# A batched Gram matrix with packed lower triangles: one TensorE loop of 43 laps, three slots to a set of banks, a group's halves consecutive, stores by 32 rows, first loads held apart

## The chip, the cores and the metric

One core of a Trainium2 chip (trn2) runs the program. The metric is the device time of one execution in microseconds (us), the median over several runs. TensorE (PE), VectorE (DVE), ScalarE (ACT) and GpSimd (POOL) compute; SyncE (SP) only issues DMAs here. The engines run their own instruction streams and meet at semaphores.

## The reference

The input is 2048 matrices of 64 rows and 256 columns (float32, 134 MB). For each matrix the kernel computes all products of pairs of rows and writes those below the diagonal, packed (2016 numbers for each matrix, 16.5 MB in all).

```python
Z = jnp.einsum('bnd,bmd->bnm', inputs, inputs)      # 2048 x 64 x 64
li, lj = jnp.tril_indices(64, k=-1)
return Z[:, li, lj]                                 # 2048 x 2016
```

## The kernel before, in words

The work goes by tiles of 16 matrices, 128 tiles in all. A tile has two sides of 8 matrices (side 0 ends on partitions 0 to 63, side 1 on 64 to 127), and each side has two slots of 4 matrices. Eight tiles make a group of 128 matrices, and there are 16 groups.

- SP (`load`, L99): one DMA of 1 MB for each tile, 128 partitions by 4 rows of 2 KB, into `x_in`, a ring of 8 tiles. The load of tile t waits until tile t-8 is turned.
- DVE (`turn`, L156): one 32x32 block transpose of a whole tile from `x_in` to `x_turned`, a ring of 3 tiles. It waits for the load and for the products of tile t-3.
- PE (`multiply`, L199): 256 matmuls for each tile, 128 for each slot (8 chunks of 32 columns by 4 quadrants by 2 sides), each preceded by its weight load. Slot s has its own four banks `slot_banks{s}`, and its next use waits until ACT has copied the last one. The first two tiles (128 % 3 = 2, `BEFORE_LOOP`) are written out ahead of a loop of 42 laps of 3 tiles.
- ACT (`keep`, L221): one copy of 128x256 from the banks to `products` for each slot; `products` holds two groups. From tile 10 on ACT also does, after each `keep`, a quarter of a piece of `pack` (L236, L239): it copies the rows of a turned group to their packed places in `packed_rows`, which has two buffers. A group has 4 pieces of 16 rows and so 16 quarters. The first quarter of a group waits until the store of the group before the last has landed (`stored`), and ACT's later `keep`s stand behind that wait.
- DVE (`turn_rows`, L170): four transposes of 128x1024 for each group, `PIECE_LAG` = 10 tiles and more behind, from `products` to `row_halves`.
- POOL (L141): 62 small copies for each group, 31 rows by 2 sides, that carry the columns from 32 on across 32 partitions; before its last two pieces are done SP can't store.
- SP (`store`, L105, L110): after the load of tile 8g+28 (`STORE_LAG`) it waits for ACT and POOL and issues four DMAs of 252 KB for group g, one for each run of 32 positions and each side. Stores and loads stand in one queue. The rows of y that belong to one side of a tile are 8 consecutive ones, and then 8 of the other side follow, so a store is written as

```python
rows = y[first:first + BLOCK * SIDES].rearrange("(t s u) c -> s t u c", s=SIDES, u=PER_SIDE)
sync.dma_start(rows[side], packed_rows[side * HALF:side * HALF + BLOCK, buffer, run])
```

with t = 4 as its outermost dimension and u = 8 under it.

Of the kernel before, what the change touches and what calls it, by code (L numbers as in the profile page):

```python
# [7 lines left out]
PARTS = 128  # L8
# [11 lines left out]
def gram_lower_triangle(nc: bass.Bass, x: bass.AP, y: bass.AP):  # L20
# [5 lines left out]
    TILE = QUADRANTS * SIDES * SLOTS  # L26
    TILES = BATCHES // TILE
    PER_SIDE = QUADRANTS * SLOTS
    IN_RING = 8
    RING = 3  # L30
    BANKS = 4
    ARRAY_TILES = QUADRANTS * SIDES


    BEFORE_LOOP = TILES % RING
    LATE_CHUNK = CHUNKS - 2


    GROUP_TILES = 8
    GROUP = GROUP_TILES * TILE  # L40
    GROUPS = TILES // GROUP_TILES
    KEPT = GROUP // SIDES
    RUNS = KEPT // BLOCK
    PIECES = 4
    PIECE = ROWS // PIECES
# [3 lines left out]
    PIECE_LAG = GROUP_TILES + 2  # L49
    STORE_LAG = PIECE_LAG + 2 * PIECES + 2 + IN_RING  # L50
# [4 lines left out]
    with ExitStack() as stack:  # L55
# [3 lines left out]
        def semaphore(name):  # L59
# [3 lines left out]
        x_turned = sbuf("x_turned", [PARTS, RING, SIDES * SLOTS, CHUNKS, ROWS])  # L63
        products = sbuf("products", [PARTS, 2, ROWS, KEPT])
# [4 lines left out]
        banks = [stack.enter_context(nc.psum_tensor(f"slot_banks{s}", [PARTS, BANKS, 8, ROWS], F32))  # L69
                 for s in range(SLOTS)]  # L70

        loaded = [semaphore(f"loaded{k}") for k in range(IN_RING)]
        turned = [semaphore(f"turned{j}") for j in range(RING)]
        multiplied = [semaphore(f"slot_multiplied{s}") for s in range(SLOTS)]
        kept = [[semaphore(f"kept{j}_{s}") for s in range(SLOTS)] for j in range(RING)]
        rows_turned = semaphore("rows_turned")
        packed_home = semaphore("packed_home")
        packed_across = semaphore("packed_across")
        stored = [semaphore(f"stored{b}") for b in range(2)]

        block = stack.enter_context(nc.Block())


        turned_ahead = [RING if j >= BEFORE_LOOP else 0 for j in range(RING)]
        kept_ahead = [(turned_ahead[j], RING if j + 1 >= BEFORE_LOOP else 0) for j in range(RING)]

        def turned_value(t):
            return turned_ahead[t % RING] + (t // RING + 1) * RING

        def kept_value(t, slot):  # L90
            return kept_ahead[t % RING][slot] + (t // RING + 1) * RING

        @block.sync
        def _(sync):
            def load(t):
                k = t % IN_RING
                if t >= IN_RING:
                    sync.wait_ge(turned[(t - IN_RING) % RING], turned_value(t - IN_RING))
                sync.dma_start(x_in[:, k], x_pairs[t * TILE * BLOCK:(t + 1) * TILE * BLOCK].rearrange(  # L99
                    "(k p) e -> p k e", p=PARTS)).then_inc(loaded[k], 16)  # L100

            def store(group):
                buffer = group % 2
                sync.wait_ge(packed_home, (group + 1) * PIECES)
                sync.wait_ge(packed_across, (group + 1) * (PIECES // 2))  # L105
                for run in range(RUNS):
                    first = group * GROUP + run * BLOCK * SIDES
                    rows = y[first:first + BLOCK * SIDES].rearrange("(t s u) c -> s t u c", s=SIDES, u=PER_SIDE)
                    for side in range(SIDES):
                        sync.dma_start(rows[side], packed_rows[side * HALF:side * HALF + BLOCK, buffer, run]).then_inc(  # L110
                            stored[buffer], 16)

            for t in range(TILES):
                load(t)
                group, behind = divmod(t - STORE_LAG, GROUP_TILES)
                if group >= 0 and behind == 0:
                    store(group)
            for group in range((TILES - 1 - STORE_LAG) // GROUP_TILES + 1, GROUPS):
                store(group)
            for b in range(2):  # L120
                sync.wait_ge(stored[b], (GROUPS - b + 1) // 2 * SIDES * RUNS * 16)

        @block.gpsimd
        def _(pool):
            for j in range(RING):
                if turned_ahead[j]:
                    pool.sem_inc(turned[j], turned_ahead[j])
                for slot in range(SLOTS):
                    if kept_ahead[j][slot]:
                        pool.sem_inc(kept[j][slot], kept_ahead[j][slot])  # L130

            for group in range(GROUPS):
                buffer = group % 2
                if group >= 2:
                    pool.wait_ge(stored[buffer], group // 2 * SIDES * RUNS * 16)
                for piece in range(PIECES // 2, PIECES):
                    pool.wait_ge(rows_turned, group * PIECES + piece + 1)  # L137
                    for i in range(max(BLOCK + 1, piece * PIECE), (piece + 1) * PIECE):
                        for side in range(SIDES):
                            first = side * HALF  # L140
                            last = nc.gpsimd.tensor_copy(  # L141
                                packed_rows[first:first + BLOCK, buffer, :,
                                            first_column(i) + BLOCK:first_column(i) + i],
                                row_halves[first + BLOCK:first + HALF, i, :, 0:i - BLOCK])
                    last.then_inc(packed_across, 1)

        @block.vector
        def _(dve):
            def turn(t):


                k, j = t % IN_RING, t % RING
                dve.wait_ge(loaded[k], (t // IN_RING + 1) * 16)
                if t >= RING:
                    dve.wait_ge(multiplied[SLOTS - 1], (t - RING + 1) * ARRAY_TILES)  # L155
                nc.vector.transpose(  # L156
                    x_turned[:, j].rearrange("p k c (i r) -> p k r c i", r=JOINED),
                    x_in[:, k].rearrange("p k (r c d) -> p k r c d", r=JOINED, c=CHUNKS)).then_inc(turned[j], RING)

            def turn_rows(group, piece):  # L160
                rows = slice(piece * PIECE, (piece + 1) * PIECE)
                if piece == 0:
                    last = (group + 1) * GROUP_TILES - 1
                    dve.wait_ge(kept[last % RING][SLOTS - 1], kept_value(last, SLOTS - 1))
                if group > 0:

                    dve.wait_ge(packed_home, (group - 1) * PIECES + piece + 1)  # L167
                    if piece >= PIECES // 2:
                        dve.wait_ge(packed_across, (group - 1) * (PIECES // 2) + piece - PIECES // 2 + 1)
                nc.vector.transpose(  # L170
                    row_halves[:, rows].rearrange("p i h j -> p (i h) j"),
                    products[:, group % 2, rows, :].rearrange("p i (h q) -> p (i h) q", q=BLOCK)).then_inc(
                    rows_turned, 1)

            for t in range(TILES):
                turn(t)
                group, behind = divmod(t - PIECE_LAG, GROUP_TILES)
                if group >= 0 and behind % 2 == 0:
                    turn_rows(group, behind // 2)
            for n in range((TILES - 1 - PIECE_LAG) // 2 + 1, GROUPS * PIECES):  # L180
                turn_rows(n // PIECES, n % PIECES)

        @block.tensor
        def _(pe):
            def multiply(j, step, first_of_all=False):


                pe.wait_ge(turned[j], step)
                for slot in range(SLOTS):
                    if slot > 0 and not first_of_all:  # L190
                        pe.wait_ge(kept[(j - 1) % RING][slot], step)
                    for c in range(CHUNKS):
                        if slot == SLOTS - 1 and c == LATE_CHUNK:

                            pe.wait_ge(kept[j][0], step)
                        for g in range(QUADRANTS):
                            for side in range(SIDES):
                                rows = x_turned[g * BLOCK:(g + 1) * BLOCK, j, side * SLOTS + slot, c, :]
                                done = nc.tensor.matmul(  # L199
                                    banks[slot][side * HALF:(side + 1) * HALF, g, 0, :], rows, rows,  # L200
                                    start=c == 0, stop=c == CHUNKS - 1)
                                if c == CHUNKS - 1:
                                    done.then_inc(multiplied[slot], 1)

            for t in range(BEFORE_LOOP):
                multiply(t, RING, first_of_all=t == 0)
            laps = TILES // RING
            with pe.Fori(2 * RING, (laps + 2) * RING, RING) as step:
                for n in range(RING):
                    multiply((BEFORE_LOOP + n) % RING, step)  # L210

        @block.scalar
        def _(act):
            def keep(t, slot):
                group, in_group = divmod(t, GROUP_TILES)
                if group >= 2 and in_group == 0 and slot == 0:

                    act.wait_ge(rows_turned, (group - 1) * PIECES)
                act.wait_ge(multiplied[slot], (t + 1) * ARRAY_TILES)  # L219
                first = in_group * PER_SIDE + slot * QUADRANTS  # L220
                nc.scalar.copy(products[:, group % 2, :, first:first + QUADRANTS],  # L221
                               banks[slot][:, :, 0, :].rearrange("p g i -> p i g")).then_inc(kept[t % RING][slot], RING)

            def pack(n, quarter):

                group, piece = divmod(n, PIECES)
                buffer = group % 2
                if piece == 0 and quarter == 0 and group >= 2:
# [40 lines left out]
```

## Time and profile before

| | |
|---|---|
| median of 3 runs | 545.54 us (545.45, 545.54 and 549.28) |
| profiled execution, its own time | 549.26 us |
| its span, first to last instruction | 547.5 us |
| PE / weight loads / DVE / ACT / POOL busy | 417.1 / 408.4 / 359.7 / 206.5 / 202.9 us |
| granted TensorE clock, mean | 0.903 of full speed |
| moved by DMA | 151.09 MB, 276 GB/s over the span |

The busy times are sums over the whole span, which has three stretches with different limits: the first 60 us, the tiles after them, and the last 36 us, in which PE has nothing to do. PE's busy time is modelled and says little of how fast it goes; the distance between laps is the better measure.

### The profile page before, as it was taken

The numbers are of one execution on the slowest core, as the hardware profiler recorded it, in microseconds if no ns is written. First come the engines' busy times: TensorE is split into PE (matmuls) and PEld (weight loads), VectorE is DVE, ScalarE is ACT, GpSimd is POOL, SyncE is SP. The second block draws the span as 40 slices with busy tenths as digits, with TensorE's granted clock in tenths as the row PEclk, the third lists the DMA queues.
The fourth block names the chain that finished last, engine by engine and source line by source line (L and its number), as shares of the span: only waits on it lengthen the run. The fifth ranks groups of instructions, "written<-read, shape, count | busy, mean of one in ns | idle before, by whom it ended". The sixth has DMA issues, their size and how long they took to land.

```text
span 547.5 us, 68554 instructions
## 1 busy us (share of the span) xinstructions
PE 417.1 (76%) x32768; PEld 408.4 (75%) x32768; DVE 359.7 (66%) x192; ACT 206.5 (38%) x1009; POOL 202.9 (37%) x996
## 2 busy tenths in 40 slices
PE   2345799999999895969779695978969596997300
PEld 2335799999999895969779695978969595997300
DVE  4213489999898593949669393967949395785300
ACT  1001125554555452534344352435435252443710
POOL 0000006372826080624417071442608053361880
PEclk9999999999999997988979798897979798797755
DMA  8982499999796997979798897969799797974011
GB/s 312 386 305 88 167 349 331 325 320 341 270 351 244 331 329 264 339 244 360 239 339 302 286 335 257 331 231 365 281 308 322 245 332 284 328 261 161 25 75 76
DMA packets 69921, 151.09 MB, mean 276 GB/s; under 512 B 2304, under 2 KB 2304, under 8 KB 69888
## 3 DMA queue, kind: packets, MB, share of 16 engines
q1 hardware_dynamic: 69888, 150.74, 78.0%
q8 instruction: 10, 0.16, 0.1%
q14 instruction: 23, 0.19, 0.1%
HBM read 134.22 MB, written 16.52 MB: 275 GB/s over the span
## 4 chain that ended last, share of the span: by engine, by line
DMA 36%; PE 36%; SPq 9%; issue 7%; POOL 5%; DVE 3%; ACT 2%; POOLq 0%; DVEq 0%; ACTq 0%
PE slot_banks L199 36%; DMA y_dram<-packed_rows 22%; DMA x_in<-x_dram 14%; POOL packed_rows L141 5%; SPq L110 4%; SPq L99 4%; DVE x_turned L156 3%; ACT packed_rows L236 1%; ACT products L221 1%; DVE row_halves L170 1%; POOLq L55 0%; DVEq L155 0%; ACTq L219 0%; DVEq L167 0%; POOLq L137 0%
## 5 line engine op out<-in xcount | busy, mean ns | idle before, releaser
L199 PE MATMUL slot_banks<-x_turned 32*64 32x64 f32 x32768 | 417.1, 247 | 93.8 <-ACT products L221 52.5
L199 PEld LDWEIGHTS slot_banks<-x_turned 32*64 32x64 f32 x32768 | 408.4, 140 | 102.3 <-ACT products L221 54.0
L156 DVE STREAM_TRANSPOSE x_turned<-x_in 128x2048 f32<-128x2048 f32 x128 | 291.0, 2289 | 152.9 <-DMA x_in<-x_dram 65.8
L141 POOL COPY packed_rows<-row_halves 32x2 f32<-32x2 f32 (+30 forms) x992 | 202.7, 204 | 331.9 <-DVE row_halves L170 291.8
L221 ACT COPY products<-slot_banks 128x256 f32<-128x256 f32 x256 | 95.2, 372 | 235.8 <-PE slot_banks L199 235.8
L236 ACT COPY packed_rows<-row_halves 128x2 f32<-128x2 f32 (+30 forms) x496 | 71.2, 220 | 67.5 <-DMA y_dram<-packed_rows 67.4
L170 DVE STREAM_TRANSPOSE row_halves<-products 128x1024 f32<-128x1024 f32 x64 | 76.9, 1203 | 8.6 <-POOL packed_rows L141 4.9
L239 ACT COPY packed_rows<-row_halves 128x128 f32<-128x128 f32 x256 | 63.2, 303 | 1.9 <-DVE row_halves L170 1.9
L221 ACT ACT_TABLE_LOAD x1 | 1.3, 1283 | 11.2 <-PE slot_banks L199 11.2
L263 POOL MEMSET const-float32-0.0<- 128x1 f32 x1 | 0.1, 98 | 0.2 <-issue 0.2
L263 POOL MEMSET const-bfloat16-1.0<- 128x1 bf16 x1 | 0.1, 101 | 0.0
L263 POOL MEMSET const-uint8-127<- 128x1 uint8 x1 | 0.1, 99 | 0.0
L263 POOL MEMSET const-float32-1.0<- 128x1 f32 x1 | 0.1, 98 | 0.0
## 6 DMA issues: line engine op xcount, KB each, us to landing
x_in<-x_dram SPq DMA_DIRECT2D x128, 1024.0 KB, 15.4
y_dram<-packed_rows SPq DMA_DIRECT2D x64, 252.0 KB
```

The lines of the kernel that those rows point to most:

```text
L99: sync.dma_start(x_in[:, k], x_pairs[t * TILE * BLOCK:(t + 1) * TILE * BLOCK].rearrange("(k p) e -> p k e", p=PARTS)).then_inc(loaded[k], 16)
L110: sync.dma_start(rows[side], packed_rows[side * HALF:side * HALF + BLOCK, buffer, run]).then_inc(stored[buffer], 16)
L141: last = nc.gpsimd.tensor_copy(packed_rows[first:first + BLOCK, buffer, :, first_column(i) + BLOCK:first_column(i) + i], row_halves[first ...
L156: nc.vector.transpose(x_turned[:, j].rearrange("p k c (i r) -> p k r c i", r=JOINED), x_in[:, k].rearrange("p k (r c d) -> p k r c d", r=J ...
L170: nc.vector.transpose(row_halves[:, rows].rearrange("p i h j -> p (i h) j"), products[:, group % 2, rows, :].rearrange("p i (h q) -> p (i ...
L199: done = nc.tensor.matmul(banks[slot][side * HALF:(side + 1) * HALF, g, 0, :], rows, rows, start=c == 0, stop=c == CHUNKS - 1)
L221: nc.scalar.copy(products[:, group % 2, :, first:first + QUADRANTS], banks[slot][:, :, 0, :].rearrange("p g i -> p i g")).then_inc(kept[t ...
L236: last = nc.scalar.copy(packed_rows[:, buffer, :, at:at + i], row_halves[:, i, :, 0:i])
L239: last = nc.scalar.copy(two[:, :, :, 0:BLOCK], row_halves[:, i:i + 2].rearrange("p w h j -> p h w j"))
L263: nc = bacc.Bacc("TRN2", target_bir_lowering=False, num_devices=1)
```

## The change

PE's program becomes one loop of 43 laps of three tiles. As 43 times 3 is 129, the first lap begins with a blank tile that DVE fills with zeros. The banks are now two sets of four; the six slots of a lap are put in them three by three (`SET_SLOTS` = 3), and ACT copies a set at once (or in two copies, where a group ends inside it). `products` holds three groups instead of two. A tile now has 8 matrices of the first half of its group and 8 of the second half, so one side of a group is 64 consecutive matrices: a load is two DMAs of 512 KB, and a store of a group is two DMAs of 64 rows of y, written with 32 as outermost dimension. Among the first loads, those of tiles 2, 3 and 4 wait until the load before has landed. Pieces go from the last rows to the first. `PIECE_LAG` goes from 10 to 11, a piece's packing from 21 slots behind to 23, `STORE_LAG` from 28 to 30. In the last group DVE carries side 1 across and POOL only side 0; POOL packs the 15 shortest rows; and the group is stored in two parts, rows 32 to 63 first.

```diff
+    APART = range(2, 5)
+    LAP = 3
+    LAPS = -(-TILES // LAP)
+    BLANK = LAPS * LAP - TILES
+    SETS = 2
+    SET_SLOTS = LAP * SLOTS // SETS
...
+    KEPT_RING = 3
...
-    PIECE_LAG = GROUP_TILES + 2
-    STORE_LAG = PIECE_LAG + 2 * PIECES + 2 + IN_RING
+    PIECE_LAG = GROUP_TILES + 3
+    PACK_LAG = 2 * PIECE_LAG + 1
+    STORE_LAG = PIECE_LAG + 2 * PIECES + 3 + IN_RING
...
                 if t >= IN_RING:
-                    sync.wait_ge(turned[(t - IN_RING) % RING], turned_value(t - IN_RING))
-                sync.dma_start(x_in[:, k], x_pairs[t * TILE * BLOCK:(t + 1) * TILE * BLOCK].rearrange(
-                    "(k p) e -> p k e", p=PARTS)).then_inc(loaded[k], 16)
...
+                    lap, j = place(t - IN_RING)
+                    sync.wait_ge(turned[j], (lap + 1) * LAP)
+                elif t in APART:
+
+                    sync.wait_ge(loaded[t - 1], SIDES * 16)
+                group, in_group = divmod(t, GROUP_TILES)
+                for side in range(SIDES):
+                    first = (group * GROUP + side * KEPT + in_group * PER_SIDE) * BLOCK
+                    sync.dma_start(x_in[:, k, side * SLOTS:(side + 1) * SLOTS],
+                                   x_pairs[first:first + PER_SIDE * BLOCK].rearrange("(k p) e -> p k e", p=PARTS)
+                                   ).then_inc(loaded[k], 16)
+
+            def store(group, columns):
+                for side in range(SIDES):
+                    first = group * GROUP + side * KEPT
+                    sync.dma_start(y[first:first + KEPT, columns].rearrange("(h q) c -> q h c", q=BLOCK),
+                                   packed_rows[side * HALF:side * HALF + BLOCK, group % 2, :, columns]).then_inc(
+                        stored[group % 2], 16)
...
+            group, long_rows = GROUPS - 1, first_column(BLOCK)
+            sync.wait_ge(packed_home, group * PIECES + LONG_PIECES)
+            sync.wait_ge(packed_across, (group + 1) * LONG_PIECES)
+            sync.wait_ge(last_carried, 1)
+            store(group, slice(long_rows, PACKED))
+            sync.wait_ge(packed_home, GROUPS * PIECES - 1)
+            sync.wait_ge(last_packed, 1)
+            store(group, slice(0, long_rows))
...
+            for j in range(BLANK):
+                nc.vector.memset(x_turned[:, j], 0.0).then_inc(turned[j], LAP)
...
+            for i in range(BLOCK + 1, ROWS):
+                last = carry_across(nc.vector.tensor_copy, GROUPS - 1, i, 1)
+            last.then_inc(last_carried, 1)
...
+                for slot in range(SLOTS):
+                    s, at = divmod(j * SLOTS + slot, SET_SLOTS)
+                    if s == 1 and at == 0:
+                        pe.wait_ge(kept[1], step)
                     for c in range(CHUNKS):
-                        if slot == SLOTS - 1 and c == LATE_CHUNK:
...
+                        if j == LAP - 1 and slot == SLOTS - 1 and c == CHUNKS - 2:
+
+                            pe.wait_ge(kept[0], step)
...
-            for t in range(BEFORE_LOOP):
-                multiply(t, RING, first_of_all=t == 0)
-            laps = TILES // RING
-            with pe.Fori(2 * RING, (laps + 2) * RING, RING) as step:
-                for n in range(RING):
-                    multiply((BEFORE_LOOP + n) % RING, step)
...
+            with pe.Fori(LAP, (LAPS + 1) * LAP, LAP) as step:
+                for j in range(LAP):
+                    multiply(j, step)
...
+                    if group >= KEPT_RING and in_group == 0:
+
+                        act.wait_ge(rows_turned, (group - KEPT_RING + 1) * PIECES)
```

## Rows read from the trace of the kernel before

**Rows 1.** The page, 40 slices of the span, busy tenths of PE and DMA.
```profile
PE   2345799999999895969779695978969596997300
DMA  8982499999796997979798897969799797974011
```

**Rows 2.** Chain that ended last, 60 to 165 us: start us, us, what.
```profile
69.39 9.06 PE slot_banks L199 x413
...
78.60 9.13 PE slot_banks L199 x433
...
87.89 9.06 PE slot_banks L199 x415
```

**Rows 3.** The page, groups of instructions: busy us, mean ns | idle before, releaser.
```profile
L156 DVE STREAM_TRANSPOSE x_turned<-x_in 128x2048 f32<-128x2048 f32 x128 | 291.0, 2289 | 152.9 <-DMA x_in<-x_dram 65.8
L141 POOL COPY packed_rows<-row_halves 32x2 f32<-32x2 f32 (+30 forms) x992 | 202.7, 204 | 331.9 <-DVE row_halves L170 291.8
L221 ACT COPY products<-slot_banks 128x256 f32<-128x256 f32 x256 | 95.2, 372 | 235.8 <-PE slot_banks L199 235.8
...
L170 DVE STREAM_TRANSPOSE row_halves<-products 128x1024 f32<-128x1024 f32 x64 | 76.9, 1203 | 8.6 <-POOL packed_rows L141 4.9
```

**Rows 4.** Windows: stretch, length, PE, PEld, DVE, ACT, POOL, PEclk, DMA share, GB/s.
```profile
10.00:30.00 20.00, 8.28 (x482) 7.84 (x477) 6.16 (x4) 2.46 (x5) 0.00 (x0) 1.00 1.05 389
...
70.00:100.00 30.00, 29.57 (x2533) 29.18 (x2520) 27.73 (x15) 13.12 (x62) 12.07 (x60) 1.00 0.98 342
...
174.50:177.50 3.00, 3.00 (x281) 3.00 (x265) 2.39 (x2) 1.55 (x7) 0.60 (x3) 1.00 0.26 108
185.00:195.00 10.00, 9.23 (x796) 8.96 (x781) 9.64 (x6) 5.24 (x30) 3.77 (x21) 1.00 1.03 378
...
245.00:250.00 5.00, 5.00 (x341) 5.00 (x332) 3.01 (x2) 1.97 (x13) 0.00 (x0) 0.50 1.00 356
```

**Rows 5.** Loads issued at 62 to 88 us (ns of SP, landing), then 178 to 199 us.
```profile
L99 SPq DMA_DIRECT2D x_in<-x_dram x9: 367/368/368, 62.3 to 87.7; - x9
...
DMA to landing us min/median/max: 5.2/5.3/6.3
...
DMA to landing us min/median/max: 14.0/16.9/21.7
```

**Rows 6.** Waits of PE and of ACT, whole span: us, times, longest.
```profile
PE slot_banks L199 <- ACT products L221: 52.5, 11, 5.8
...
ACT packed_rows L236 <- DMA y_dram<-packed_rows: 67.4, 11, 7.2
```

**Rows 7.** The page, DMA packets of the span, and the queue of PE's code.
```profile
DMA packets 69921, 151.09 MB, mean 276 GB/s; under 512 B 2304, under 2 KB 2304, under 8 KB 69888
...
q8 instruction: 10, 0.16, 0.1%
```

**Rows 8.** Timeline of PE in the first 60 us: start, us, group [idle before].
```profile
8.71 3.73 PE L199 MATMUL slot_banks<-x_turned 32*64 32x64 f32 x223 [8.71 <-DVE x_turned L156]
...
16.18 2.35 PE L199 MATMUL slot_banks<-x_turned 32*64 32x64 f32 x128 [3.74 <-issue]
...
43.79 2.34 PE L199 MATMUL slot_banks<-x_turned 32*64 32x64 f32 x128 [1.39 <-issue]
...
58.81 11.40 PE L199 MATMUL slot_banks<-x_turned 32*64 32x64 f32 x860 [3.29 <-issue]
```

**Rows 9.** Timeline of the end, 499 us on.
```profile
499.64 11.20 PE L199 MATMUL slot_banks<-x_turned 32*64 32x64 f32 x865
...
504.69 30.37 POOL L141 COPY packed_rows<-row_halves 32x2 f32<-32x2 f32 x124 [15.51 <-DVE row_halves L170]
...
513.92 3.79 ACT L236 COPY packed_rows<-row_halves 128x2 f32<-128x2 f32 x31
517.62 1.69 ACT L239 COPY packed_rows<-row_halves 128x128 f32<-128x128 f32 x8
...
535.15 3.61 SPq L110 DMA_DIRECT2D y_dram<-packed_rows  x4
```

More of the change, by code:

```diff
@@ L97, in load, with store_whole @@
                 if t >= IN_RING:
-                    sync.wait_ge(turned[(t - IN_RING) % RING], turned_value(t - IN_RING))
-                sync.dma_start(x_in[:, k], x_pairs[t * TILE * BLOCK:(t + 1) * TILE * BLOCK].rearrange(
-                    "(k p) e -> p k e", p=PARTS)).then_inc(loaded[k], 16)
-            def store(group):
-                buffer = group % 2
-                sync.wait_ge(packed_home, (group + 1) * PIECES)
[L105 to L111, printed above, removed]
+                    lap, j = place(t - IN_RING)
[14 more added lines that the diff above has]
+                        stored[group % 2], 16)
+            def store_whole(group):
+                sync.wait_ge(packed_home, (group + 1) * PIECES)
+                sync.wait_ge(packed_across, (group + 1) * LONG_PIECES)
+                store(group, slice(0, PACKED))
             for t in range(TILES):
@@ L124, in _ @@
         def _(pool):
[L125 to L130, printed above, removed]
+            pool.sem_inc(kept[1], LAP)
             for group in range(GROUPS):
[L133 to L136, printed above, removed]
+                last_group = group == GROUPS - 1
+                wait_packed_free(pool, group)
+                for piece in range(LONG_PIECES):
@@ L137, in _ @@
                     pool.wait_ge(rows_turned, group * PIECES + piece + 1)
[L138 to L144, printed above, removed]
@@ L145, in _ @@
-                    last.then_inc(packed_across, 1)
+                    rows = piece_rows(piece)
+                    for i in range(max(BLOCK + 1, rows.start), rows.stop):
+                        for side in range(1 if last_group else SIDES):
+                            last = carry_across(nc.gpsimd.tensor_copy, group, i, side)
+                    last.then_inc(packed_across, 1)
+            pool.wait_ge(packed_across, GROUPS * LONG_PIECES)
+            pool.wait_ge(rows_turned, GROUPS * PIECES)
@@ L147, in _ @@
+            rows = piece_rows(PIECES - 1)
+            for i in range(1, rows.stop):
+                last = pack_short(nc.gpsimd.tensor_copy, GROUPS - 1, i)
+            last.then_inc(last_packed, 1)
         @block.vector
@@ L157, in turn, with turn_rows @@
                     x_turned[:, j].rearrange("p k c (i r) -> p k r c i", r=JOINED),
[L158 to L161 removed]
+                    x_in[:, k].rearrange("p k (r c d) -> p k r c d", r=JOINED, c=CHUNKS)).then_inc(turned[j], LAP)
+            def turn_rows(n):
+                group, piece = divmod(n, PIECES)
+                rows = piece_rows(piece)
@@ L175, in _ @@
+            turned_rows = 0
             for t in range(TILES):
                 turn(t)
[L177 to L181, printed above, removed]
+                if t >= PIECE_LAG and (t - PIECE_LAG) % 2 == 0:
+                    turn_rows(turned_rows)
+                    turned_rows += 1
@@ L212, in _ @@
         @block.scalar
         def _(act):
[L214 to L228, printed above, removed]
-                    act.wait_ge(stored[buffer], group // 2 * SIDES * RUNS * 16)
+            def keep(lap, s):
+                act.wait_ge(half_multiplied if s == 0 else tile_multiplied[LAP - 1], (lap + 1) * ARRAY_TILES)
+                begin = (lap * SETS + s) * SET_SLOTS - BLANK * SLOTS
+                slot, end = max(0, begin), begin + SET_SLOTS
+                while slot < end:
+                    group, in_group = divmod(slot, GROUP_SLOTS)
+                    count = min(end - slot, GROUP_SLOTS - in_group)
+                    if group >= KEPT_RING and in_group == 0:
+                        act.wait_ge(rows_turned, (group - KEPT_RING + 1) * PIECES)
+                    last = nc.scalar.copy(
+                        products[:, group % KEPT_RING, :, in_group * QUADRANTS:(in_group + count) * QUADRANTS].rearrange(
+                            "p i (m g) -> p i m g", g=QUADRANTS),
+                        bank_sets[s][:, :, slot - begin:slot - begin + count, :].rearrange("p g m i -> p i m g"))
+                    slot += count
+                last.then_inc(kept[s], LAP)
@@ L230, in pack @@
+            def pack(n):
+                group, quarter = divmod(n, PIECES * 4)
+                piece, quarter = divmod(quarter, 4)
+                if piece == 0 and quarter == 0:
+                    wait_packed_free(act, group)
                 if quarter == 0:
-                    act.wait_ge(rows_turned, n + 1)
-                first = piece * PIECE + quarter * (PIECE // 4)
+                    act.wait_ge(rows_turned, group * PIECES + piece + 1)
+                first = piece_rows(piece).start + quarter * (PIECE // 4)
@@ L241, in pack @@
                 if quarter == 3:
                     last.then_inc(packed_home, 1)
-            behind = 0
-            for t in range(TILES):
-                for slot in range(SLOTS):
-                    keep(t, slot)
-                    if 2 * t + slot > 2 * PIECE_LAG:
-                        pack(behind // 4, behind % 4)
-                        behind += 1
-            for n in range(behind, GROUPS * PIECES * 4):
-                pack(n // 4, n % 4)
+            n = 0
+            for lap in range(LAPS):
+                for s in range(SETS):
+                    keep(lap, s)
+                    while n + PACK_LAG < (lap * SETS + s + 1) * SET_SLOTS - BLANK * SLOTS:
+                        pack(n)
+                        n += 1
@@ L256 @@
+            for n in range(n, (GROUPS * PIECES - 1) * 4):
+                pack(n)
 def kernel(r_inputs):
```

106 lines of the change are left out of this document (62 added, 44 removed).

## The prediction

> **What bounds the kernel now.** I began with the slices of the page [rows 1]: PE is half idle in the first four slices, full in the next nine, and then dips at even distances to the end; in the last three it does nothing. So there are three stretches, each to be read by itself.
>
> *The full stretch* shows what PE can do. On the chain of work that ended last, laps of three tiles start at 69.39, 78.60 and 87.89 us [rows 2]: 9.21 and 9.29 us, 3.07 to 3.10 us for a tile. Two tiles and one `turn_rows` cost DVE 2 x 2.29 + 1.20 = 5.8 us against 6.1 of PE, and two `keep`s cost ACT 0.74 [rows 3]. PE is the bound there, and the DMA engines follow it with 342 GB/s [rows 4]; a load lands 5.3 us after its issue, so the input ring is full [rows 5].
>
> *The dips*: PE waits 52.5 us for ACT's copies, and ACT waits 67.4 us, 11 times, for a store to land before it may pack [rows 6]. Why does a store land late? While stores are moved, the DMA share is 0.26 and the rate 108 GB/s, against 1.03 and 378 GB/s beside it [rows 4]. A quarter of the engines works, four of sixteen, and the loads behind stand still. The packet count says the same: 2304 small packets [rows 7] are 128 loads x 16 + 64 stores x 4. The outermost dimension is 128 for a load and 4 for a store. A group's four stores, 1.03 MB, at 108 GB/s take 9.6 us; on sixteen engines, at four times that, 2.4 us. Over this the loads fall behind, they land 17 us after issue [rows 5], and the store in the same queue does too. PE idles, comes back at half its clock (0.50, the 1.2 GHz level [rows 4]) and loses some more.
>
> *The start*: PE runs 223 matmuls, stops 3.74 us, then runs 128 at a time in 2.35 us with stops of 1.39 to 4.3 us that nothing in the trace releases; there are 9 from 12.44 to 58.81 us, and then none [rows 8]. 128 matmuls and their weight loads are 256 instructions, half a tile. PE's queue of code has 10 pieces, 0.16 MB, thus 16 KB each [rows 7], which is 64 bytes for each of those 256. Two written-out tiles and a first lap of three are ten half tiles. So each stop is code arriving once.
>
> *The end*: PE is done at 510.84. POOL carries 124 rows from 504.69 to 535.06, SP issues the last stores until 538.76, and the span ends at 547.5 [rows 9]: 36.7 us behind PE.
>
> **The change part by part.**
>
> 1. *Start.* Code for three tiles instead of five: 6 half tiles. The 223 matmuls that PE has at once are 1.75 of them, so 4.25 must come, in five pieces. PE needs no input for the blank tile: the memset of 2048 elements isn't in the trace; it lies between nothing and a transpose of the same tile, 2.3 us, and I take 2 (it is the same size), so PE starts at about 3 us and runs dry at 3 + 3.7 = 6.7 [rows 8]. A piece costs its 2.35 us plus a stop: 1.39 with little traffic, 3.3 around a single load, 3.7 to 4.3 under full traffic [rows 8]. Loads 2 to 4 are held apart, so I take 3.3 for three stops, 4 for two: 6.7 + 3 x 3.3 + 2 x 4 + 4 x 2.35 + 0.6 = 34.6, call it 34 us for the end of lap 1, with two real tiles done. All stops cheap give 6.7 + 5 x 1.4 + 10 = 24, all dear 38. The price of holding apart is idle DMA time: three lone loads at 5.3 us instead of some 2.7 [rows 4, 5], 8 us. PE's code covers it: load 1 is there at 8 us, load 4 at 8 + 3 x 5.3 = 24, load 8 at 24 + 4 x 2.7 = 35, while PE at 34 us needs only the third tile.
>
> 2. *Middle.* 42 laps remain. With the stores at 32 outermost rows I take sixteen engines, the even split, as the row of the loads has it; the other bound is four, as now (a rival below). DMA work of a group: eight loads of 1 MB at 378 to 389 GB/s [rows 4], 21.6 to 22.2 us, plus 2.4 us: 24.0 to 24.6, against 8 x 3.07 to 3.10 = 24.6 to 24.8 of PE. That is hardly less, but PE is still the longer, and the ring holds eight tiles. So PE's lap of 9.21 to 9.29 stays: 42 x 9.24 = 388 us. The clock stays full when no wait breaks it, as in 70 to 100 us.
>  The Trainium skill, page "DMA: Bandwidth & Descriptors", section "Why a DMA increments its semaphore by 16 and not by 1", says that a DMA uses the largest number of engines up to 16 that divides the outermost dimension on both sides. By that rule the old store gets four and the new one sixteen; the trace agrees for 4 and 128, and no run so far shows 32.
>
>  *Waits added or moved.* Two load DMAs for a tile: SP spends 0.37 us on one of 1 MB [rows 5], so at most 0.74, under 3.07; SP isn't late. `keep` for three slots: 128x768 isn't in the trace; between 0.37 (one slot) and 3 x 0.37 = 1.12 us [rows 3]; I take 0.75, two-thirds of it being elements. Either is under the three slots, 4.6 us, in which the other set fills, and ACT's total falls or stays. The store of group g is issued after load 8g+30, at about PE's tile 21.4 of those counted from 8g, as ACT finishes packing near 21; behind SP's wait stand loads 8g+31 and on, at most 2 tiles late, while the ring holds 8: hidden, unless the queue is empty and DMA has no spare, which leads to the second rival. ACT's packing of group g+2 needs the store when tile 28 to 29 is kept: 6.6 to 7.6 tiles or 20 to 23 us after issue. In a short queue a store lands in 5.3 us, in a deep one in 17 to 22 [rows 5]. So this wait goes where PE is the bound. What is late next is PE itself. The third buffer of `products` takes away a wait that the trace doesn't show as a cost: nothing. Blank tile: in the first lap, counted.
>
> 3. *End*, from PE's last matmul on (E). ACT copies the last set, E + 0.8, and then has 22 quarters of packing: of group 14 the last 4 long copies (L239) and 31 short ones (L236), of group 15 16 and 16, at 1.69/8 = 0.21 and 3.79/31 = 0.12 us each [rows 9]: 20 x 0.21 + 47 x 0.12 = 9.8, E + 11. POOL takes (30.37 us for 124 copies, with a wait; 0.204 each plus a gap, 0.25 [rows 3, 9]) until about E + 2.5 for group 14, then 31 copies of side 0, 7.8 us, then 15 short rows, 3.6 us: E + 14. DVE has four `turn_rows` (E + 7.5, each waiting for ACT's piece) and 31 copies; such copies on DVE aren't in the trace, so between nothing and POOL's 0.25 us each, I take ACT's 0.12, the nearest row: E + 11.3. So the long rows' store is issued at E + 11.3 and the short rows' at E + 14, two issues at 3.61/4 = 0.9 us each [rows 9], and it lands some 2.6 later, what a lone load takes beyond its bytes: E + 18. Bounds: E + 14 to E + 23. Before it was 36.7: the gain is 31 carries off POOL, no four-engine store at the end, and less in the last store.
>
> **Sum.** 34 + 388 + 18 = 440 us of span. The profiled execution before had 547.5 of span in 549.26 of its own time, 1.8 more: 442. That execution lay 3.7 above the median of its three runs, where the other two are; the changed kernel should have less of such waiting, so I take half of it off: 440 us, about -19%. By part: start, lap 1's end and the tiles done set against each other, (60.9 - 5 x 3.08) - (34 - 2 x 3.08) = 17.7; end 18.7; the rest, 71, in the middle.
>
> **Rivals.**
>
> - *The DMA engines become the bound* (0.18). For it: 342 GB/s already at a share of 0.98 in the stretch where they only follow PE [rows 4], so the spare may be far less than 389 suggests; stores add to it. 150.7 MB at 342 GB/s are 441 us, plus 5 for the start, minus 6 for stores that fall in the end, plus a transpose and a tile's products 5, plus 18: 463. Against: 378 GB/s for 10 us in the middle, with full use of PE and DVE. It decides from where eight loads take more than 24.7 - 2.4 us, which is 376 GB/s, near to the 378 of [rows 4]; every 10 GB/s below cost some 10 us in all, so the first of them lie within the forecast's own range.
>  The Trainium skill, same page, section "Specifications", gives some 358 GB/s of HBM for a core; an estimate by it would be 421 us for the bytes and some 443 in all. The rows of 378 and 389 GB/s speak against it as a limit of a core alone.
> - *ACT still waits for stores* (0.08). The landing, not the bandwidth, sets it: if it takes over 6.6 tiles, each of 12 groups waits. Half the present 6.1 us [rows 6] for each is 37: 477.
> - *Stores stay on four engines* (0.05): the change then doesn't do what it says. The middle keeps its present (510.84 - 60.9)/123 = 3.66 us a tile: 34 + 126 x 3.66 + 18 = 513.
> - *Slower than before* (0.03): a pair of half loads isn't overlapped with its neighbours as one whole load is, because the queue admits so many DMAs, not so many bytes. A lone load takes 5.3 us [rows 5]; at that for a tile the middle is 126 x 5.3 = 668, in all 720. It decides from (547.5 - 34 - 18)/126 = 3.9 us a tile. Against it: now loads stand six deep, so that three would do.
>
> **How the numbers follow.** The forecast has 0.66: 440, its own range 426 to 455 from start 24 to 38, laps of 9.18 to 9.4, end 14 to 23. With the first two rivals 0.92 is covered up to 480, and the low end of all bounds together is 424. Under 1% is what a measurement of this kernel can't tell from no change; no case lies there, 0.02 is kept for it, 0.03 for slower.
>
> **What would show it.** Start: PE's code queue with about 6 pieces, not 10; PE busy from about 3 us; steady laps from 24 to 38 us. Middle: laps 9.2 us apart to the end, clock 1.00, no slice near 0.26 of DMA share, small packets as many as 256 x 16 for loads and 16 for each of some 34 stores; ACT's wait for stores near zero. If DMA bounds: DVE waits for loads throughout, share near 1, landing 15 us and more. End: 18 us behind PE. The prediction is wrong if stores of 32 rows don't spread, or if PE's lap with three slots in one bank isn't the lap of before: the trace can't show that.

## The result and the profile after

The changed kernel takes 437.28 us (436.77 to 437.67, 4 runs) against 545.5 us, a ratio of 0.800 (0.797 to 0.804). The forecast was 440. The profiled execution has 435.9 us of span.

The page of the changed kernel, 40 slices of the span; they answer to [rows 1], a slice now being 10.9 us:

```profile
PE   4569999999999999999998999989899998989810
...
DMA  5589999999999999999999999999999999999416
```

The first line is the row of busy tenths of PE, the second that of DMA. The dips at even distances are gone from both. DMA is at 9 from the fourth slice to the 37th without a break, which it never was for long before, and PE has small gaps in the second half. The same page, counts and queues (to [rows 7]), and groups of instructions (to [rows 3]):

```profile
DMA packets 72378, 151.01 MB, mean 346 GB/s; under 512 B 4640, under 2 KB 4768, under 8 KB 72352
...
q8 instruction: 6, 0.10, 0.1%
...
L282 ACT COPY products<-bank_set 128x768 f32<-128x768 f32 (+2 forms) x96 | 69.0, 729 | 215.4 <-PE bank_set L256 204.9
...
L122 DVE COPY packed_rows<-row_halves 32x2 f32<-32x2 f32 (+30 forms) x31 | 3.5, 191 | 0.0
L225 DVE MEMSET x_turned<- 128x2048 f32 x1 | 1.8, 1765 | 1.2 <-PEq L325 1.2
```

4640 small packets are 256 x 16 for the loads and 34 x 16 for the stores: every DMA now ends on sixteen engines. Six pieces of code come instead of ten.

The timeline of PE at the start (to [rows 8]); the bracket is the idle time before:

```profile
3.05 3.70 PE L256 MATMUL bank_set<-x_turned 32*64 32x64 f32 x222 [3.05 <-DVE x_turned L225]
...
9.89 2.35 PE L256 MATMUL bank_set<-x_turned 32*64 32x64 f32 x128 [3.14 <-issue]
...
27.83 17.42 PE L256 MATMUL bank_set<-x_turned 32*64 32x64 f32 x1384 [2.85 <-issue]
```

The laps after it, on the chain from 30 to 70 us (to [rows 2]):

```profile
38.41 8.78 PE bank_set L256 x425
47.19 0.12 issue
47.31 8.78 PE bank_set L256 x424
```

A lap takes 8.90 us here, against 9.21. Counted back from the one that starts at 38.41 - 8.90, lap 1 ends at 29.5 us. The waits of the whole span (to [rows 6]), and windows with the columns of [rows 4]:

```profile
PE bank_set L256 <- DVE x_turned L203: 10.7, 14, 1.8
...
DVE x_turned L203 <- DMA x_in<-x_dram: 41.5, 15, 4.2
...
ACT packed_rows L117 <- DMA y_dram<-packed_rows: 15.9, 9, 3.6
...
POOL packed_rows L122 <- DMA y_dram<-packed_rows: 132.5, 13, 10.8
```

```profile
30.00:60.00 30.00, 29.59 (x2564) 29.20 (x2555) 24.36 (x13) 4.80 (x6) 4.97 (x24) 1.00 1.05 389
60.00:200.00 140.00, 138.08 (x12097) 135.97 (x12091) 132.49 (x71) 65.86 (x309) 71.04 (x349) 1.00 1.04 385
200.00:300.00 100.00, 94.72 (x8269) 92.72 (x8261) 87.30 (x48) 45.11 (x215) 50.71 (x248) 1.00 1.02 371
...
424.00:427.00 3.00, 0.00 (x0) 0.00 (x0) 2.97 (x11) 2.91 (x19) 3.00 (x21) 0.50 1.00 239
```

PE no longer waits for ACT at all. It waits for DVE, and DVE for loads (12 of the 41.5 us lie in the first 60 us, the others behind them): the DMA engines have become the bound, at 385 to 389 GB/s first and 371 later. The eight tiles loaded ahead hide it until 169 us, where DVE's first wait for a load stands on the chain. And the end (to [rows 9]):

```profile
407.54 20.07 POOL L122 COPY packed_rows<-row_halves 32x32 f32<-32x32 f32 x93 [10.22 <-DMA y_dram<-packed_rows]
...
412.50 2.95 PE L256 MATMUL bank_set<-x_turned 32*64 32x64 f32 x256 [1.05 <-DVE x_turned L203]
```

PE is done at 415.45, and 20.4 us follow. From lap 1's end that makes (415.45 - 29.5)/42 = 9.19 us a lap on average.

### The profile page after: what moved, and what is told of

Read it like the earlier page. It is cut to its first block, busy times and chain, and to the rows that moved or that the text cites. A ratio compares the mean times of both kernels' runs of the same rounds, so it can differ in the third digit from the quotient of the medians.

```text
span 435.9 us, 68822 instructions
## 1 busy us (share of the span) xinstructions
PE 385.4 (88%) x33024; PEld 377.5 (87%) x33024; DVE 363.7 (83%) x224; ACT 179.3 (41%) x834; POOL 197.2 (45%) x980
## 2 busy tenths in 40 slices
DMA packets 72378, 151.01 MB, mean 346 GB/s; under 512 B 4640, under 2 KB 4768, under 8 KB 72352
## 4 chain that ended last, share of the span: by engine, by line
PE 35%; DMA 28%; DVE 16%; SPq 10%; issue 6%; POOL 3%; ACT 0%; DVEq 0%; POOLq 0%
PE bank_set L256 35%; DMA x_in<-x_dram 25%; DVE x_turned L203 12%; SPq L138 9%; DVE row_halves L219 3%; DMA y_dram<-packed_rows 3%; POOL packed_rows L122 3%; DVE packed_rows L122 1%; DVE x_turned L225 0%; SPq L145 0%; ACT packed_rows L117 0%; ACT products L282 0%; DVEq L202 0%; DVEq L218 0%; DVEq L64 0%
## 5 line engine op out<-in xcount | busy, mean ns | idle before, releaser
L256 PE MATMUL bank_set<-x_turned 32*64 32x64 f32 x33024 | 385.4, 237 | 30.0 <-issue 12.1
L256 PEld LDWEIGHTS bank_set<-x_turned 32*64 32x64 f32 x33024 | 377.5, 132 | 37.8 <-issue 21.9
L203 DVE STREAM_TRANSPOSE x_turned<-x_in 128x2048 f32<-128x2048 f32 x128 | 290.6, 2286 | 58.0 <-DMA x_in<-x_dram 41.5
L122 POOL COPY packed_rows<-row_halves 32x60 f32<-32x60 f32 (+30 forms) x961 | 194.9, 204 | 232.3 <-DMA y_dram<-packed_rows 132.5
L282 ACT COPY products<-bank_set 128x768 f32<-128x768 f32 (+2 forms) x96 | 69.0, 729 | 215.4 <-PE bank_set L256 204.9
L117 ACT COPY packed_rows<-row_halves 128x128 f32<-128x128 f32 x256 | 56.4, 300 | 17.4 <-DMA y_dram<-packed_rows 15.9
L111 ACT COPY packed_rows<-row_halves 128x32 f32<-128x32 f32 (+30 forms) x481 | 62.3, 220 | 0.0
L122 DVE COPY packed_rows<-row_halves 32x2 f32<-32x2 f32 (+30 forms) x31 | 3.5, 191 | 0.0
L225 DVE MEMSET x_turned<- 128x2048 f32 x1 | 1.8, 1765 | 1.2 <-PEq L325 1.2
L111 POOL COPY packed_rows<-row_halves 128x2 f32<-128x2 f32 (+14 forms) x15 | 2.1, 195 | 0.1
```

The lines of the kernel that those rows point to most:

```text
L111: return copy(packed_rows[:, group % 2, :, at:at + i], row_halves[:, i, :, 0:i])
L117: return copy(two[:, :, :, 0:BLOCK], row_halves[:, i:i + 2].rearrange("p w h j -> p h w j"))
L122: return copy(packed_rows[first:first + BLOCK, group % 2, :, at + BLOCK:at + i], row_halves[first + BLOCK:first + HALF, i, :, 0:i - BLOCK])
L203: nc.vector.transpose(x_turned[:, j].rearrange("p k c (i r) -> p k r c i", r=JOINED), x_in[:, k].rearrange("p k (r c d) -> p k r c d", r=J ...
L225: nc.vector.memset(x_turned[:, j], 0.0).then_inc(turned[j], LAP)
L256: done = nc.tensor.matmul(bank_sets[s][side * HALF:(side + 1) * HALF, g, at, :], rows, rows, start=c == 0, stop=c == CHUNKS - 1)
```

## The experiments

Times are medians of four runs; ratios are to the kernel before on the same chip. For the changed kernel it is 0.800 (0.797 to 0.804).

**Stores on four engines again** (`e_store4`).

```diff
-                    sync.dma_start(y[first:first + KEPT, columns].rearrange("(h q) c -> q h c", q=BLOCK),
-                                   packed_rows[side * HALF:side * HALF + BLOCK, group % 2, :, columns])...
+                    for run in range(RUNS):
+                        rows = y[first + run * BLOCK:first + (run + 1) * BLOCK, columns]
+                        sync.dma_start(rows.rearrange("(u t) c -> t u c", t=4),
+                                       packed_rows[side * HALF:side * HALF + BLOCK, group % 2, run, columns])...
```

> The changed kernel, but each store is four DMAs with 4 as outermost dimension, as before the change (the 32 rows of a run land in y in another order; all else is computed as it was). Theory A, the spread of the stores over the engines is what the middle gained: the stretches with a DMA share near 0.25 come back for about 9.6 us in each group, ACT waits some 60 us for stores, and the time is 500 to 520 us, against 437. Theory B, the middle gained from the third products buffer, the longer lags and PE's loop, and the engines of a store matter little: 437 to 450 us.

520.67 us, ratio 0.952 (0.947 to 0.956): theory A, just above its upper end. The dips are back in PE's row, and a window shows the quarter share:

```profile
PE   4369999999999695987959699595987959699300
...
226.00:228.00 2.00, 2.00 (x211) 2.00 (x196) 0.00 (x0) 0.00 (x0) 0.00 (x0) 1.00 0.25 105
...
ACT packed_rows L117 <- DMA y_dram<-packed_rows: 69.9, 11, 7.6
```

ACT's wait for stores is 69.9 us in 11 times, as before the change. The third buffer of `products` and the longer lags don't prevent it.

**The kernel before with stores by 32 rows** (`b_spread`). Only `load` and `store` are taken from the change, with their counts.

```diff
-                for run in range(RUNS):
-                    first = group * GROUP + run * BLOCK * SIDES
-                    rows = y[first:first + BLOCK * SIDES].rearrange("(t s u) c -> s t u c", s=SIDES, u=PER_SIDE)
-                    for side in range(SIDES):
-                        sync.dma_start(rows[side], packed_rows[side * HALF:side * HALF + BLOCK, buffer, run])...
+                for side in range(SIDES):
+                    first = group * GROUP + side * KEPT
+                    sync.dma_start(y[first:first + KEPT].rearrange("(h q) c -> q h c", q=BLOCK),
+                                   packed_rows[side * HALF:side * HALF + BLOCK, buffer])...
```

> The kernel before, but a tile has 8 matrices of each half of its group, so that a group is stored by two DMAs with 32 as outermost dimension; PE's program, lags, the banks and the end are as before. Theory A: nearly all of the middle's gain is here, 545 - 73 = 472 us, with laps of 9.2 us and no PE stop longer than 2 us after the start; the end a few us shorter as well, so 462 to 478. Theory B: 530 to 545 us.

465.5 us, ratio 0.851 (0.847 to 0.855): theory A. Row of PE, two waits and the last stretch of PE:

```profile
PE   2336599999999999999999999999999999999500
...
PE slot_banks L202 <- issue: 26.2, 14, 4.1
PE slot_banks L202 <- DVE x_turned L159: 8.4, 1, 8.4
...
416.70 18.25 PE L202 MATMUL slot_banks<-x_turned 32*64 32x64 f32 x1536 [0.17 <-issue]
```

After the start PE never stops for longer than the 0.1 to 0.2 us between laps; it is done at 434.95, and the span of 463.4 ends 28.5 us later. So the stores, with the order of tiles that they need, give some 80 of the 108 us, and the rest of the change 28. The traces tell where these 28 lie. On the chain of this run PE has eight tiles done and begins a lap here:

```profile
67.36 9.07 PE slot_banks L202 x413
```

The changed kernel is that far at 47.31, 20.1 us earlier; it is 19.5 us ahead at PE's last matmul, and its end is 8.0 us shorter (20.4 against 28.5). The start gives 20 us, the end 8, and the laps between give nothing.

**The first lap written out ahead of the loop** (`e_ahead`): 12 half tiles of code instead of 6.

```diff
+            for j in range(LAP):
+                multiply(j, LAP)
-            with pe.Fori(LAP, (LAPS + 1) * LAP, LAP) as step:
+            with pe.Fori(2 * LAP, (LAPS + 1) * LAP, LAP) as step:
```

> The changed kernel with the first lap written out ahead of the loop, so that PE's code is 12 half tiles instead of 6. Theory A, each half tile of code met for the first time costs a stop: 12 pieces in the code queue, steady laps start after some 49 instead of 29 us. As DMA is the bound and loads what it can meanwhile, most of these 20 us but not all reach the end: 8 to 18 us slower. Theory B, the stops at the start come from the first use of banks or from waits, not from code: no change.

457.26 us, 20 more than the changed kernel, ratio 0.836 (0.830 to 0.842). The stops run on to 61 us, and the code queue has twice the pieces:

```profile
q8 instruction: 12, 0.20, 0.2%
...
61.18 14.04 PE L256 MATMUL bank_set<-x_turned 32*64 32x64 f32 x1066 [2.57 <-issue]
...
72.23 8.78 PE bank_set L256 x424
...
430.56 2.95 PE L256 MATMUL bank_set<-x_turned 32*64 32x64 f32 x256 [0.72 <-DVE x_turned L203]
```

Code it is (A), but the 20 us lie above the 8 to 18 expected, because the delay was larger than the 20 us assumed. The last two lines are a lap on the chain and PE's last stretch. Counted back from the lap at 72.23, the first two laps end at 63.3 us, against 38.4 in the profiled execution of the changed kernel: 24.9 us later. PE's last matmul is 18.1 us later, so some 7 us were made up on the way. How much is made up depends on what it is compared with: beside `a_again` (below), the same program as the changed kernel with a slower start, the two distances are 19.8 and 19.3 us.

**The last group as the others** (`e_tail`): POOL carries both sides, DVE none.

> The changed kernel, but in the last group POOL carries both sides and DVE none. POOL has 31 more copies of 0.25 us before it packs the short rows: the end is 6 to 8 us longer, the rest the same, 443 to 445. If another engine sets the end (ACT with its 22 quarters), less than 3 us.

445.35 us, 8 more, ratio 0.814 (0.808 to 0.820), just above the 443 to 445 expected; POOL's last stretch has 124 copies instead of 93.

```profile
406.21 30.37 POOL L122 COPY packed_rows<-row_halves 32x32 f32<-32x32 f32 x124 [10.20 <-DMA y_dram<-packed_rows]
```

The 8 us are those by which the end of `b_spread` is longer. That 437.3 + 20 + 8 also makes the 465.5 us of `b_spread` is in part chance: `e_ahead` has 12 pieces of code and starts PE at 3 us, `b_spread` has the ten of before and starts PE at 8.5 us.

**More increments** (`e_inc6`): the slots that have none at their end increment a semaphore that nobody reads.

```diff
                                     elif at == SET_SLOTS - 1:
                                         done.then_inc(half_multiplied, 1)
+                                    else:
+                                        done.then_inc(unread, 1)
```

> The changed kernel with 16 more semaphore increments in a lap (48, as before the change, instead of 32), on a semaphore that nobody waits for. Theory A, the increments of the last matmuls are why an unhindered lap takes 8.90 us instead of the 9.21 before: the lap becomes 9.2 us, 19 ns for an increment; the total hardly moves, by 0 to 4 us, as DMA takes over as the bound. Theory B, the 5 instead of 9 waits in a lap or the banks' layout made it shorter: the lap stays at 8.90.

438.13 us, ratio 0.801 (0.797 to 0.805), the same time. The chain shows the lap of before again, 9.19 us:

```profile
47.57 9.06 PE bank_set L257 x414
56.64 0.12 issue
56.76 9.06 PE bank_set L257 x414
...
DVE x_turned L204 <- DMA x_in<-x_dram: 21.6, 9, 3.6
```

So theory A: 16 increments cost 0.29 us, 18 ns each; neither the waits nor the layout of the banks had shortened the lap. The last line is from this run's waits of DVE. PE itself waits for no tile after its start here and keeps its laps of 9.19 us to the end, and yet the time is the same: with 48 increments PE's own pace is what the loads allow, and with 32 it is faster than that to no use.

**Fewer bytes** (`e_less`): of every other tile from the ninth on, side 1 is loaded only by half; old contents stand in for the rest.

> The changed kernel, but of every other tile from the ninth on a quarter of the rows isn't loaded (the old contents are used), 15 MB less in 120 tiles. Theory A, from about 30 us on the DMA engines are the bound and PE only spends the eight tiles loaded ahead: laps stay at 8.90 to the end, DVE's waits for loads (41.5 us) go, and the time falls by some 12 us, to 423 to 427. Theory B, PE's later stops come from the order of waits between the engines, not from the rate: laps lengthen after 169 us all the same, 433 to 438.

427.62 us, ratio 0.781 (0.775 to 0.786), some 10 less. PE keeps its lap to the end of the work:

```profile
374.22 8.80 PE bank_set L257 x424
383.14 8.80 PE bank_set L257 x423
```

PE's waits for DVE are gone and DVE's for loads are 6.0 us. The 6.0 us all lie in the first 60 us. Theory A; its 423 to 427 is just missed. In the profiled execution the first lap ended some 5 us later than in the one of the changed kernel; whether that is the reason wasn't tried.

**Three buffers of packed rows, two of products** (`e_packed3`), in the same memory.

```diff
-    KEPT_RING = 3
+    KEPT_RING = 2
+    PACKED_RING = 3
```

(and `group % PACKED_RING` for `packed_rows` and `stored`.)

> The changed kernel with three buffers of packed_rows and two of products (the same memory), so that ACT and POOL wait for the store of three groups back. Theory A, the end is 20.4 us instead of 18 because POOL's last two groups start only when the store of group 12 has landed (at 407.54), behind the deep queue of loads: POOL's waits for stores (132 us) go, group 14 is carried before PE ends, the end falls to 13 to 16 us and the time by 4 to 8. The products buffer given up costs nothing or stops of 1 us in a group. Theory B, the third products buffer matters, as ACT must wait for turned rows: slower by 5 us or more.

433.15 us, ratio 0.791 (0.785 to 0.797), 4 less: theory A. The interval just touches that of the changed kernel; `c1_inc1` below, with the same buffers and fewer increments, is clear of `a_again`. POOL's waits and PE's and POOL's last stretches:

```profile
POOL packed_rows L123 <- DVE row_halves L220: 190.5, 16, 55.7
...
413.50 2.95 PE L257 MATMUL bank_set<-x_turned 32*64 32x64 f32 x256 [0.86 <-DVE x_turned L204]
...
418.93 4.70 POOL L123 COPY packed_rows<-row_halves 32x32 f32<-32x32 f32 x31 [3.09 <-DVE row_halves L220]
```

POOL waits for no store any more, and the span of 432.6 ends 16.2 us behind PE. ACT waits 3.4 us in all for turned rows, since the third buffer of `products` is gone.

**All first loads at once** (`e_noapart`): `APART = range(0)`.

> The changed kernel with the first loads all issued at once. Theory A, the DMA engines are the bound from 30 us on and the 3 x 3.7 us of DMA time given up at the start are missing at the end: the first lap ends some 8 us later (stops of 3.7 to 4.3 us instead of 1.1 to 3.1), yet the time falls by 1 to 5 us. Theory B, PE is the bound, so a later first lap is a later end: slower by 6 to 9 us.

439.38 us, ratio 0.803 (0.799 to 0.807) against 0.800 (0.797 to 0.804): no difference that can be told, and neither expectation holds. Two windows of this kernel, and DVE's waits for loads:

```profile
0.00:30.00 30.00, 11.46 (x650) 10.70 (x657) 11.01 (x5) 1.66 (x2) 0.20 (x4) 1.00 0.97 358
30.00:60.00 30.00, 25.80 (x2116) 25.34 (x2110) 17.89 (x8) 4.25 (x6) 0.00 (x0) 1.00 0.81 287
...
DVE x_turned L203 <- DMA x_in<-x_dram: 19.8, 9, 3.2
```

The loads move 358 instead of 219 GB/s in the first 30 us, but in the next 30 us 287 instead of 389, for the ring of eight is full while PE waits for its code. By 60 us that is 19.4 MB against 18.2: 3 us of loading won. PE's first lap ended at 35.52 + 10.46 - 8.79 = 37.2 us by its stretch on the chain, 7.7 later. Most of it isn't missing at the end: PE, and DVE behind it, start later, and DVE then waits 19.8 us for loads instead of 41.5. The two effects nearly cancel; none was tried alone.

**The three last together**, beside the changed kernel once more (`a_again`). `c1_inc1` is `e_packed3` with one increment at the end of a slot (4 in a lap); `c2_inc1_noapart` is that with all first loads at once; `c3_two_apart` has

```diff
-    APART = range(2, 5)
+    APART = range(2, 8)
-                    sync.wait_ge(loaded[t - 1], SIDES * 16)
+                    sync.wait_ge(loaded[t - 2], SIDES * 16)
```

> The changed kernel as it is, once more, beside the next three: 437 us. No theory says otherwise.

> Three buffers of packed_rows and two of products, and one increment instead of eight at the end of a slot (4 in a lap instead of 32). Theory A, an increment costs TensorE some 18 us in a thousand laps' parts, that is 0.28 us for 16 in a lap: with 28 fewer the unhindered lap falls from 8.90 to 8.4 us, but the DMA engines are the bound from lap 2 on, so the time stays at 432 to 434, as with the three buffers alone. Theory B, PE's rate still sets the time: 42 x 0.5 = 20 us less, 412 to 418.

> As the one before, with the first loads issued at once. Theory A, PE now has room to catch up the 8 us by which its first lap ends later, so what the loads gain at the start reaches the end: 424 to 430 us. Theory B, the time lost at the start is PE's and is not given back: 438 to 442.

> As the one before, but loads 2 to 7 each wait for the load of two tiles earlier, so that two are in flight. Theory A, the engines stay busy and PE's code still comes a little faster than with all at once: 424 to 430 us. Theory B, a code piece is delayed by any load in flight, however few: stops as with all at once and the same time as the one before within 2 us.

| kernel | us | ratio to before |
|---|---|---|
| a_again | 436.04 | 0.795 (0.793 to 0.797) |
| c1_inc1 | 432.97 | 0.789 (0.787 to 0.792) |
| c2_inc1_noapart | 435.78 | 0.794 (0.792 to 0.796) |
| c3_two_apart | 431.68 | 0.787 (0.785 to 0.789) |

`c1_inc1`: the lap fell to 8.46 us, as the chain shows, and the time stayed at that of `e_packed3`. That is A's core, PE's rate doesn't set the time; the 20 us of B didn't come.

```profile
40.32 8.34 PE bank_set L257 x445
48.66 0.12 issue
48.78 8.35 PE bank_set L257 x447
```

`c2_inc1_noapart`: even with a lap 0.44 us shorter, loading at once gained nothing; by the medians it lost 3 us, but the intervals touch. Both expectations are missed, A's 424 to 430 and B's 438 to 442. `c3_two_apart` is faster than `c2_inc1_noapart` and than the changed kernel, the latter by 1%, and lies between its two expectations. Most of that 1% is there in `c1_inc1` already, from which it differs only in the first loads: it is 1.3 us faster than that, and the intervals overlap. So two loads in flight are not shown to be better than one. Its windows:

```profile
0.00:30.00 30.00, 12.44 (x734) 11.49 (x735) 11.01 (x5) 1.66 (x2) 0.20 (x4) 0.68 0.89 311
30.00:60.00 30.00, 27.67 (x2374) 27.26 (x2373) 21.96 (x11) 5.21 (x7) 1.89 (x10) 0.87 1.03 379
```

Two loads in flight move 20.7 MB by 60 us, more than one (18.5 in `c1_inc1`) or all (19.5 in `c2_inc1_noapart`). PE's code is in by 34 us, against 32 and 38. More is loaded than with one load in flight and the code comes earlier than with all of them; that this is why it beats loading all at once is argued from the windows, not tried by itself.

## Why the prediction was right, point by point

- *Stores on a quarter of the engines bound the middle*: shown from both sides, by 80 us when only the stores and the order of tiles are changed and by 83 when only the stores are undone. The forecast put 18 us on the start, 19 on the end and 71 on the middle. Its 60.9 us for the end of PE's first lap in the kernel before should be 60.2, counted back from the lap that starts at 69.39 [rows 2]. The spans then show (60.2 - 5 x 3.08) - (29.5 - 2 x 3.08) = 21 for the start, 36.7 - 20.4 = 16 for the end, and of the 111.6 us in all 74 for the middle.
- *PE's lap of 9.21 to 9.29 stays; PE is still the longer*: wrong, and that the sum held all the same is luck. The lap fell to 8.90 us, because I left out the 16 increments that the change drops; `e_inc6` shows it. DMA at 385 GB/s needs 9.42 MB / 385 GB/s = 24.5 us for a group, PE 8/3 laps of 8.90, 23.7 us, and so the rival of the DMA engines came true in part: it had 0.18 and 463 us, and it costs 10 to 12 us (`e_less`). 24.5 us for a group are 9.18 us for a lap, which happens to be what PE would have taken with the increments of before (9.19, `e_inc6`, 438.13 us): the two bounds lie at the same place, and so 42 laps came to 386 us, forecast 388, under the other bound. The condition I had named, loads at 378 against 376 GB/s, was a knife's edge, and PE's side of it was misjudged.
- *A group's stores take 2.4 us on sixteen engines*: mis-sized. With no loads beside them the two stores of a group move 239 GB/s (window 424 to 427 us), that is 4.3 us; four engines move 108 [rows 4]. Four times the engines gave 2.2 times the rate. Among loads it costs less: in the 140 us from 60 us on, with five groups' stores, the rate stays at 385 GB/s.
- *Start, 34 us*: 29.5 in the profiled execution, where stops were 1.1 to 3.1 us, and 34.6 in that of `a_again`, whose time is no longer. Six pieces of code and their stops are as forecast, and `e_ahead` shows the cause.
- *Holding the first loads apart is covered by PE's code*: right in that loading all at once is no faster (`e_noapart`). The DMA engines could have moved more meanwhile (`c3_two_apart`, 20.7 MB by 60 us against 18.5 in `c1_inc1`), but no gain in time from it is shown.
- *Waits of ACT for stores go*: 67.4 to 15.9 us, and none reaches PE. What I missed is POOL behind the same store: it began group 14 at 407.54, so that group was carried by 422.8, E + 7.3 instead of E + 2.5, and DVE waited 5.0 us for it. Hence an end of 20.4 us instead of 18; `e_packed3` takes this away and has 16.2.
- *POOL's 31 carries*: 8 us by `e_tail`, forecast 7.8. DVE's copies took 3.49 us for 31, forecast 0.12 us each.
- *A `keep` of three slots*: 0.80 us for a full one, 0.73 on average with the shorter ones, forecast 0.75. *The memset*: 1.77 us, forecast 2. *Half loads as a queue's burden*, the rival on the slower side: no sign of it, 389 GB/s with halves.
- The Trainium skill, page "DMA: Bandwidth & Descriptors", section "Why a DMA increments its semaphore by 16 and not by 1", says that a DMA uses the largest number of engines up to 16 that divides the outermost dimension on both sides. The trace agrees for 32 too: 4640 small packets, sixteen for each DMA. The section "Specifications" of that page of the Trainium skill gives some 358 GB/s of HBM for a core; this core alone moved 385 GB/s over 140 us, so it isn't a limit here.

## What to carry to other kernels

Look at the outermost dimension of every DMA: one of 4 kept twelve engines idle and everything queued behind it waiting, which the profile shows as a DMA share of 0.25 in short windows. When two bounds lie within a few per cent of each other, work out both anew for the changed program, the semaphore increments too; removing work from the one then only uncovers the other. And test a forecast that came true: here its number was right and the bound behind it was not. Code met for the first time costs as well: a loop that begins at once, with a blank tile for which no load is needed, was worth 20 us here.

## What the hardware showed that I had not expected

- The two stores of a group, each from 32 partitions and on sixteen engines, ran at 239 GB/s together with no loads beside them, against 108 on four engines and 385 to 389 for loads. Whether the 32 partitions or the writes limit it wasn't tried.
- An increment on a matmul costs TensorE 16 to 18 ns: laps of 9.19, 8.90 and 8.46 us with 48, 32 and 4 of them.
- The same start had stops of 1.1 to 3.1 us in one execution and 2.8 to 4.0 in another of the same program, and the total differed by only 1 us.
- After 200 us the rate falls from 385 to 371 GB/s at nearly the same share (1.04, 1.02). The slowest slices of 10 us after 200, 339 to 347 GB/s, have shares of 0.98 to 0.99, so the engines were a little less busy there. What causes that stays open; with all first loads at once the rate was 374 before and after 200 us.
